# Scores of a graph-attention kernel: keys carried through the folded query matrix instead of a query projection

## The reference, cut to what matters

```python
q_exp = where(x.sum(-1) == 0, 0, cond)             # a zero row of x drops the condition
self_feat = concat([x, q_exp]) @ W_self.T + b_self
output = self_feat
for d in range(2):
    A    = adj[:, :, :20] if d == 0 else swapaxes(adj, 1, 2)[:, :, :20]   # B, N, 20, 11
    mask, vb = A.sum(-1) > 0, A @ w_bias + b_bias
    qh = (self_feat @ Wq[d].T + bq[d])              # B, N, 16, 32
    kh = (self_feat[:, :20] @ Wk[d].T + bk[d])      # B, 20, 16, 32
    aff = einsum('bnhd,bmhd->bnhm', qh, kh) / sqrt(32)
    w = softmax(where(mask, aff, NEG) + vb)         # over the 20 keys
    output += einsum(w, self_feat[:, :20], Wout[d]) + bout[d]
out = x + relu(output)
```

## Time and profile before

| | us |
|---|---|
| time, median of 3 runs (lowest, highest) | 1905.44 (1904.07, 1905.74) |
| the profiled execution, its own time | 1906.23 |
| its span, first to last instruction | 1904.4 |
| mean granted TensorE clock | 0.999 of 2.4 GHz |

### The profile page before, as it was taken

One profiled execution on the slowest core, in us unless ns is written; L12 is line 12 of the kernel. 1 busy time (PEld: TensorE's weight loads), 2 busy tenths in 40 slices (PEclk: granted clock), 3 DMA queues, 4 the chain that ended last, 5 costly groups with the idle time before them and its releaser, 6 DMA issues.

```text
span 1904.4 us, 34516 instructions
## 1 busy us (share of the span) xinstructions
PE 1887.3 (99%) x11020; PEld 1646.9 (86%) x11020; DVE 1303.7 (68%) x1897; ACT 575.5 (30%) x1189; POOL 836.6 (44%) x746
## 2 busy tenths in 40 slices
PE   8999999999999999999999999999999999999999
PEld 6899999888888888888888888888888888888887
DVE  3433232477777777777777777777777777777776
ACT  3333232233333333333333333333333333333332
POOL 0332222354444444444444444444444444444443
PEclk9999999999999999999999999999999999999999
DMA  7123324544444444444444444444444444444431
GB/s 214 34 84 89 96 90 99 136 113 122 122 122 119 118 120 121 121 121 121 121 121 121 121 121 121 121 121 121 121 121 121 121 121 121 121 121 121 121 100 63
DMA packets 227951, 219.87 MB, mean 115 GB/s; under 512 B 58176, under 2 KB 179008, under 8 KB 223808
## 3 DMA queue, kind: packets, MB, share of 16 engines
q1 hardware_dynamic: 223440, 219.24, 42.6%
q10 hardware_dynamic: 4464, 0.02, 0.1%
HBM read 164.39 MB, written 54.79 MB: 115 GB/s over the span
## 4 chain that ended last, share of the span: by engine, by line
PE 95%; DVE 1%; DMA 0%; issue 0%; SPq 0%; POOL 0%; ACT 0%; ACTq 0%; DVEq 0%
PE bank L1517 37%; PE bank L1463 19%; PE bank L849 14%; PE bank L1451 12%; PE bank L1487 8%; PE bank L1476 4%; PE bank L857 0%; PE bank L1436 0%; DMA adj<-in_mask_BxSxSx_ik 0%; PE bank L1526 0%; DVE nodes_t L88 0%; DVE qt_main L1276 0%; SPq L650 0%; DVE nodes_t L1212 0%; POOL rc L1152 0%
## 5 line engine op out<-in xcount | busy, mean ns | idle before, releaser
L1152 POOL TENSOR_TENSOR rc<-nzb,cqg 128x512 f32<-128x512 bf16 x256 | 265.1, 1041 | 419.9 <-DVE qt_main L1276 409.3
L1451 PEld LDWEIGHTS bank<-kbd,qt_main 128*128 128x128 f32 x2048 | 243.6, 192 | 19.1 <-DVE sc L1240 13.2
L1276 DVE SCALAR_TENSOR_TENSOR qt_main<-bank,bq_all,rc 128x512 f32<-128x512 f32 x256 | 190.2, 743 | 89.0 <-PE bank L1517 89.0
L1118 POOL TENSOR_TENSOR sc<-sc,mx 128x640 f32<-128x640 f32 x128 | 163.3, 1276 | 199.1 <-DVE mx L1245 198.7
L1451 PE MATMUL bank<-kbd,qt_main 128*128 128x80 f32 x2048 | 247.4, 274 | 0.2
L1362 ACT ACTIVATE wtt<-bank 128x384 f32<-128x384 f32 (+1 forms) x256 | 111.1, 435 | 381.7 <-PE bank L1476 381.6
L1251 DVE TENSOR_REDUCE sm<-sc 128x32 f32<-128x640 f32 x128 | 104.6, 817 | 162.7 <-ACT sc L1354 162.7
L1517 PE MATMUL bank<-nodes_h,wq_h 128*128 128x512 f32 x512 | 210.1, 410 | 1.9 <-DVE qt_main L1276 1.9
L1517 PE MATMUL bank<-xh_odd,wq_h 128*128 128x512 f32 x512 | 210.5, 411 | 0.0
L1517 PE MATMUL bank<-xh_odd,wq_l 128*128 128x512 f32 x512 | 202.4, 395 | 0.0
L1517 PE MATMUL bank<-nodes_h,wq_l 128*128 128x512 f32 x512 | 202.1, 395 | 0.0
(11 more groups left out here) (130 smaller groups left out, 3816.8 us busy)
## 6 DMA issues: line engine op xcount, KB each, us to landing
rows<-in_x SPq DMA_DIRECT2D x128, 256.0 KB, 5.0
xk<-in_x SPq DMA_DIRECT2D x32, 1024.0 KB, 6.1
res<-c_dram SPq DMA_DIRECT2D x32, 1024.0 KB, 4.7
out<-res SPq DMA_DIRECT2D x128, 256.0 KB, 2.1
adj<-in_mask_BxSxSx_ik SPq DMA_DIRECT2D x32, 440.0 KB, 5.6
adj<-in_mask_BxSxSx_ik SPq DMA_DIRECT2D x128, 110.0 KB
k_dram<-kv_kst SPq DMA_DIRECT2D x64, 160.0 KB, 1.8
v_dram<-kv_vt SPq DMA_DIRECT2D x256, 40.0 KB
```

The lines of the kernel that those rows point to most:

```text
L1118: pool.tensor_tensor(s, s, mx[:, b % 2, :].unsqueeze(2).to_broadcast([P, DIRS * H, NG]), ALU.subtract).then_inc(s_shifted, 1)
L1152: pool.tensor_tensor(rc[:, c % 2, :].rearrange("p (b n) -> p b n", b=G), nzb[:, par, :].rearrange("p (b n) -> p b n", b=G), cqg[:, par, c, ...
L1276: nc.vector.scalar_tensor_tensor(out=qt[:, c, :], in0=bank[c % 2][:], scalar=bq_all[:, c:c + 1], in1=rc[:, c % 2, :], op0=ALU.add, op1=ALU ...
L1451: mm = nc.tensor.matmul(dst, qt[:, c, b * N:b * N + N], kbd[:, c, :, b * NG:b * NG + NG], start=True, stop=True)
```

## The change

Let A be the folded query matrix of a head, 32 query features x 512 features of x. Before, x goes through A and the result meets the keys. After, the keys go through A, and the result, kx, meets x itself. A key of one head has 32 features only, so its matmul uses 32 of the 128 rows of the array, a strip; four heads of one 128-feature block lie on four strips.

- **prepare_weights**: the fold is written the other way round and kept once in fp32 as a_rows (ACT writes chunks 0 and 1, DVE chunks 2 and 3), instead of as wq_h and wq_l.
- **keys_and_values**: the last half no longer loads, turns and splits group 0. SP waits for 16*C on each k_stored and loads the rows of two pairs and two key tiles; DVE turns pair 0.
- **window_loop** replaces main_loop. Its step is a slot of a pair of batches, 64 slots and some at both ends. The 2 x 16 heads are split in 4 units of 8 heads; slot t works on one unit, for a window of 8 batches (4 pairs of ages 0 to 3). Each pair thus meets all four units in four slots. Per slot PE does: 5 generate steps for the next slot's window (step 0: the constants from the condition and the bias, 41 output rows; steps 1 to 4: kx for one 128-feature chunk of x each), each of 2 x 4 fp32 matmuls of 160 columns, strip r into PSUM bank r; 8 score tiles; and for the pair of age 3 and the one before, self features, turned weights and values. ACT copies each step's 1280 columns from PSUM, DVE makes the low part of the constants.
- No query projection, no qt, no POOL condition product (L1152). The final clip goes from DVE to ACT and the last addition from DVE to POOL. The loads are per pair; x comes a third time (xs) for the row sums. Edges stay in groups of 4, one direction per slot.

```diff
 def fold(n):
-    mm = nc.tensor.matmul(bank[6 + n % 2][:], chunk_columns(w1[j], jo), wqt[:, d, j, :],
+    mm = nc.tensor.matmul(bank[6 + n % 2][:], wqt[:, d, j, c * P:c * P + P], w1[j],
...
+def generate(t, step):
+    d, hh = unit(t)
+    lo, hi = window(t)
+    if step == 0:
+        pe.wait_ge(key_loaded[t.par], 16 * (t.half + 1))
+        pe.wait_ge(zl_ready, 2 * (t.n + 1) if t.real() else 2 * PAIRS)
+        if due(t.n):
+            pe.wait_ge(gen_taken, C * t.n)
+    elif step == 1:
+        pe.wait_ge(z_low, t.n + 1)
+    else:
+        pe.wait_ge(gen_taken, C * t.n + step - 1)
+    for c in range(2):
+        o = C * d + 2 * hh + c
+        for r in range(NQ):
+            s = slice(Q * r, Q * r + Q)
+            rhs = key_tile[s, t.par, c, lo * NG:hi * NG]
+            dst = slice(c * UN + lo * NG, c * UN + hi * NG)
+            if step == 0:
+                mm = nc.tensor.matmul(low_banks[0:ZR, r, dst], zl[s, o, :], rhs, start=True, stop=True)
+            else:
+                mm = nc.tensor.matmul(low_banks[:, r, dst], a_rows[s, o, step - 1, :], rhs, start=True, stop=True)
+    mm.then_inc(pe_gen, 1)
...
 def scores(t, a):
...
+    for b in range(2):
+        w = 2 * (AGES - 1 - a) + b
...
+        for j in range(C):
...
+            mm = nc.tensor.matmul(dst, xt[:, j, p.ring + b, :], kx[:, t.par, j, :, :, w, :].rearrange("p r c m -> p c r m"), start=(j == 0), stop=False)
+        mm = nc.tensor.matmul(dst, flags[0:ZR, p.ring + b, :], zc[0:ZR, t.par, :, :, w, :].rearrange("p r c m -> p c r m"), start=False, stop=True)
...
+def constants_low(t):            # DVE
+    dve.wait_ge(z_high, t.n + 1)
...
+    nc.vector.tensor_tensor(o, generated(Q, ZR, lo, hi), o.bitcast(F32), ALU.subtract).then_inc(z_low, 1)
...
+def keys_out(t, j):              # ACT
+    act.wait_ge(pe_gen, STEPS * t.n + 2 + j)
+    lo, hi = window(t)
+    nc.scalar.activation(taken(kx[:, t.par, j], lo, hi), generated(0, P, lo, hi), ACT.Copy).then_inc(gen_taken, 1)
...
+def slot(t):                     # PE
+    soft, late, nxt = t.back(3), t.back(4), t.back(-1)
+    if soft.real():
+        scores(t, 3)
+    if has_window(nxt):
+        generate(nxt, 0)
+    if late.real():
...
+        turn_weights(late, 1, 0)
+    if t.back(2).real():
+        scores(t, 2)
+    if late.real():
+        turn_weights(late, 1, 1)
+    if has_window(nxt):
+        generate(nxt, 1)
+    if late.real():
+        values(late, 1)
+    if t.back(1).real():
+        scores(t, 1)
+    if has_window(nxt):
+        generate(nxt, 2)
+    if soft.real():
+        self_features(soft, 0, range(0, 2))
+        turn_weights(soft, 0, 0)
+        self_features(soft, 0, range(2, C))
+        turn_weights(soft, 0, 1)
+    if has_window(nxt):
+        generate(nxt, 3)
+    if t.real():
+        scores(t, 0)
...
+        flag_rows(nxt)
+    if soft.real():
+        values(soft, 0)
+    if has_window(nxt):
+        generate(nxt, 4)
+    if soft.real():
+        self_features(soft, 1, range(0, C))
...
+def slot(t):                     # DVE
+    if soft.real():
+        add_masks(t, 3)
+        maxima(t, 0)
+        maxima(t, 1)
+    if has_window(nxt):
+        constants_low(nxt)
+    if t.back(2).real():
+        add_masks(t, 2)
...
+    if t.back(1).real():
+        add_masks(t, 1)
...
+            turn_pair(dve, nxt, range(C))
+        nonzero_rows(nxt)
...
+        count_and_weigh(g, t.c % 2)
+    if t.real():
+        add_masks(t, 0)
+    if has_edges(g):
+        total_and_mask(g, t.c % 2)
```

More of the change, by code:

```diff
@@ L923, in main_loop @@
     HM = H * NG
-    NC = DIRS * C
+    NO = DIRS * C
+    EDGE = 4
+    EG = B // EDGE
+    ZR = Q + WIN + 1
     SLOTS = 4
     PARTS = ((0, 3), (3, 5))
[L927 to L947, removed]
+    STEPS = C + 1
+    assert H * WH == NW * P and NW == 5 and AGES == 4 and N == P
@@ L948, in main_loop @@
+    adj0 = sb("adj0", [P, EDGE * NG, L], I32)
+    adj1 = sb("adj1", [EDGE * NG, N, L], I32)
+    sums = sb("sums", [P, 2], F32)
+    nzf = sb("nzf", [P, WIN], F32)
     wb = sb("wb", [P, L], F32)
     bb = sb("bb", [P, 1], F32)
[L950 to L954, removed]
+    vb = sb("vb", [P, N], F32)
+    cn = sb("cn", [P, N], F32)
@@ L1000, in main_loop, with __init__, back, real @@
     wtt_ready = sem("wtt_ready")
+    c_scaled = sem("c_scaled")
     pe_self = sem("pe_self")
     pe_out = sem("pe_out")
+    out_taken = sem("out_taken")
+    clipped = sem("clipped")
     res_ready = sem("res_ready")
-    S0, S1 = bank[2], bank[3]
-    def turn_bank(part, last):
-        return bank[0] if last and part == 1 else bank[7]
+    OUT, TURN = bank[6], bank[7]
+    class Pair:
+        def __init__(self, k, c):
+            self.k, self.c = k, c
+            self.n = 4 * k + c
+            self.half = 2 * k + c // 2
+            self.par = c % 2
+            self.ring = 2 * (c % AGES)
+        def back(self, a):
+            return Pair(self.k, self.c - a)
+        def real(self):
+            return not isinstance(self.k, int) or 0 <= self.n < PAIRS
+    def ages(t):
+        return [a for a in range(AGES - 1, -1, -1) if t.back(a).real()]
+    def scored(t, a):
+        if isinstance(t.k, int):
+            earlier = sum(len(ages(Pair(0, u))) for u in range(t.n))
+            return earlier + len([o for o in ages(t) if o >= a])
+        return 4 * t.n - 2 - a
+    def has_window(t):
+        return not isinstance(t.k, int) or 0 <= t.n < PAIRS + AGES - 1
+    def window(t):
+        ws = [2 * (AGES - 1 - a) for a in ages(t)]
+        return min(ws), max(ws) + 2
+    def generated(first, last, lo, hi):
+        return low_banks[first:last, :, 0:2 * UN].rearrange("p r (c x) -> p r c x", c=2)[:, :, :, lo * NG:hi * NG]
+    def taken(home, lo, hi):
+        return home.rearrange("p r c w m -> p r c (w m)")[:, :, :, lo * NG:hi * NG]
+    def unit(t):
+        u = t.c % 4
+        return u // 2, u % 2
+    def edge_group(t):
+        return (t.n + 2) // 2 if isinstance(t.k, int) else 2 * t.k + (t.c + 2) // 2
+    def has_edges(g):
+        return not isinstance(g, int) or 0 <= g < EG
+    def slots(eng, body, first):
+        for n in range(first, 4):
+            body(Pair(n // 4, n % 4))
+        with eng.Fori(1, PAIRS // 4 - 1) as k:
+            for c in range(4):
+                body(Pair(k, c))
+        for n in range(PAIRS - 4, PAIRS + 4):
+            body(Pair(n // 4, n % 4))
     def value_pieces():
@@ L1034, in sync_program @@
[L1034 to L1047 removed]
+    PIECES = len(list(value_pieces()))
```

990 lines of the change are left out of this document (485 added, 505 removed).

## The result

The changed kernel took 2180.36 us (median of 4; 2172.94 to 2190.0) against 1905.33 for the kernel before on the same chip (1904.07 to 1905.74): ratio 1.1448, 95% interval 1.1402 to 1.1493. It is 275 us slower, where 1853 had been forecast. The profiled execution took 2179.28 us, its span 2177.4.

The account below looks back on a forecast made before the run. PE was taken to bound the kernel: 412 us to the first full slot, 61 slots of 22.7 and a tail of 55 gave a span of 1852, forecast 1853 us; the forecast's own range was 1785 to 1900.

Parts of the forecast that it names:

- The uncertain step: Generated keys on PE: 40 strip matmuls a slot, four strips at once, 2.7 us (bounds 2.7 to 10.9); weakly held.
- Rival 1: Generate steps: only two strips overlap, 1.22 us a step, slot 26.1, kernel 2060 us; 22%.
- rival 2: Generate steps: no overlap or weight loads in series, slot 28.6 to 30.9, kernel 2215 to 2355 us; 12%.
- the score tile: Scores on PE: four fp32 matmuls plus the constants, 1.28 us each, eight a slot 10.3 us (9.3 to 11.6).
- The constants matmul: In each score tile: one fp32r matmul over 41 rows, 0.106 us plus 0.085 for the type change.
- Rival 3: Ten borders between strips and whole array drain: 2.7 us for 0.4, slot 25.0, or 23.9 without loads; 14%.
- Borders of the strips: Ten borders a slot between strip matmuls and whole array: 0.4 us in all (bounds nothing to 1.65).
- kept work: PE work unchanged per slot: self features, values, transposes, flags and mask, together 9.3 us.
- Head and tail: First full slot begins at 412 us, last slots take 55; bounds for both together 25 us either way.
- rival 4: Generate steps wait for evacuation (step 1's wait, ScalarE's copies): one us a slot more, kernel 1914 us; 5%.
- break-even slot: Slot length at which the changed kernel's span equals the 1904.4 us of before: 23.56 us.
- removed work: Query projection and old scores taken off PE: 14.9 us a slot, of which 13.4 come back.

Follow-up runs that it names:

- b_rows64: Kernel before, one of the 12 self-feature matmuls per batch run over 64 of its 128 rows: 1948.7 us, ratio 1.0218.
- a_take_first: Changed kernel, VectorE takes the self features before the edge sums instead of after: 2177.99 us, ratio 1.1433.
- b_unroll: Kernel before with its groups written out, no loop: 1907.35 us, ratio 1.0006.
- a_full_take_unroll: Changed kernel with constants over 128 rows, the earlier VectorE take, and all slots written out, no loop: 1940.82 us, ratio 1.0183.
- b_rows96: Kernel before, one of the 12 self-feature matmuls per batch run over 96 of its 128 rows: 1905.63 us, ratio 0.9993.
- b_loop4: Kernel before with four groups in the loop's body, twice as long, 7 passes for 14: 1923.61 us, ratio 1.0088.
- a_loop8: Changed kernel with eight slots a pass instead of four, 6 jumps for 13: 2155.54 us, ratio 1.1313.
- a_unroll: Changed kernel with all slots written out, no loop: 2124.53 us, ratio 1.1143.
- a_const_out: Changed kernel with the constants' matmul of each score tile left out: 2035.35 us (one run).
- a_full_take: Changed kernel with constants over 128 rows and the earlier VectorE take, loop kept: 2037.03 us, ratio 1.0692.

## Why the prediction was wrong

**The uncertain step was right.** The forecast hung on whether four strips run at once; they do. A step was to take 0.55 to 0.75 us and takes 0.69 and 0.76. Rival 1 wanted 1.2, rival 2 1.7 to 2.2; both are refuted. Within the step at 1206.43 the instructions start in bunches. The timeline of PE of the kernel after, three cuts of 10 to 50 ns, at 1206.55, 1206.70 and 1206.97 (each lists what is in flight then):

```profile
1206.43 0.42 PE L1547 MATMUL low_banks<-key_tile,a_rows 32*128 32x160 f32 x4
1206.43 0.55 PE L1547 MATMUL low_banks<-key_tile,a_rows 32*128 32x160 f32 x8
1206.68 0.58 PE L1547 MATMUL low_banks<-key_tile,a_rows 32*128 32x160 f32 x11
```

Four start together, four more some 0.24 us later. The rows don't say which strip each is on, but the length settles it: 16 instructions at 0.136 on four strips are 0.544. Started in the order that rival 1 supposes, each strip's second half ahead of the next strip, they would take at least 1.22. The Trainium skill, "TensorE: Matmul & The Clock Gate", Part 3, has matmuls start and end in strict program order; if the two halves stand next to each other in the program, as rival 1 took them to, that doesn't hold here. Its 3.07x would have made the five steps an estimated 3.55; they took 3.8 with borders, and 2.37/0.76 is 3.1: here page and trace agree.

**The step that failed is the score tile.** The constants matmul was costed like a full-row one, 0.106 and a type change of 0.085. It cost about 0.43 on the mean of eight tiles (12.1/8 less 1.09); on full rows it costs 0.14 (9.8/8 less 1.09). The bounds given for the tiles, 9.3 to 11.6, did not hold 12.1. The error was one of place. Rival 3 had the mechanism, a drain at a change of array split, and looked for it only at ten borders of generate steps; the 16 borders around the constants' 41 rows were not counted. The loads show it. The timeline of PEld of the kernel after:

```profile
1204.24 0.18 PEld L1568 LDWEIGHTS bank<-zc,flags 41*128 41x128 f32 x1 [0.17 <-issue]
1204.51 1.11 PEld L1567 LDWEIGHTS bank<-kx,xt_main 128*128 128x128 f32 x8
1205.80 0.18 PEld L1568 LDWEIGHTS bank<-zc,flags 41*128 41x128 f32 x1 [0.17 <-issue]
```

The load at 1205.80 starts in the same instant as its matmul, not under the one before, and so does that at 1204.51: 0.20 us lost ahead, and 0.27 to the next start. The Trainium skill, "TensorEngine Tiling (Array Packing)", Key Properties, says that a change of tiling mode drains the engine; b_rows64 agrees, with 0.33 us for two borders. Worth 2.38 us a slot, 133 us in all. It is the largest single term, but it does not turn the sign: with it put right the kernel took 2047, still 7% more than before.

**Borders of the strips** were taken at 0.4 us a slot. Steps are 0.7 over the forecast's 3.1, and kept work, whose blocks stand next to steps, 0.6 over its 9.3 (two value blocks 2.53 for 2.29). Together that is 1.3 us, and with the 0.4 of the forecast 1.7, less than rival 3's upper end of 2.7 and near its 1.65. No experiment splits it further, so that it is the borders is argued, not shown.

**The wait for res** was not in the sum. The prediction looked at waits on generate steps only; this one is at self features of the second batch (L1580), behind total_and_mask on DVE. DVE is 50% busy: an engine with time to spare and the wrong order. It is 0.6 us in the slot shown. Taking it away brought nothing alone (a_take_first) and 10 us on full rows (2046.98 to 2037.03), with the jumps in place; without them it was not tried by itself.

**The loop jump** was no part of the prediction. The kernel before has 13 of them and they cost nothing (b_unroll), so no row there shows it; the longer body brings it in. It is 56 us alone. With the other waits gone it grew to 96: 54.9 of it is idle time, and a part of the rest is the granted clock of 0.50 behind the idle stretch.

**Head and tail** were 36 us over, outside the 25 either way. The waits of the start, timeline of PE of the kernel after:

```profile
372.84 1.09 PE L1547 MATMUL low_banks<-key_tile,a_rows 32*128 32x40 f32 x16 [8.20 <-DVE zc L1255]
386.41 1.16 PE L1547 MATMUL low_banks<-key_tile,a_rows 32*128 32x80 f32 x16 [0.82 <-ACT kx L1428]
```

Step 1 waits for DVE's low constants and the later steps for ACT's copies of the partial windows, with too little PE work beside them to hide it; this is the wait that the prediction had in rival 4. Over these waits the granted clock fell to 0.79 at 340 to 380 and 0.59 at 380 to 400. In full slots that wait hardly shows (17.6 us over L1547 in all): rival 4 is refuted for the loop.

**The sum closes.** Of the 4.7 us a slot that the change missed by, tiles are 1.8, steps and kept work 1.3, the wait for res 0.6, jumps 0.8 (13 slots of 30.3 for 26.68), and 0.3 is what ordinary slots take over the one shown. a_full_take_unroll: slot 3 starts at 427.6, 61 slots of 23.63, tail 68, 1937. It misses 1852 by 57 in the slots (borders, mostly), 16 at the start and 13 at the end. The prediction's break-even slot was 23.56 with its own ends; with these ends it is (1904.4-427.6-68)/61 = 23.10. The 14.9 us of removed work per slot come back almost in full: 9.8 and 3.9 us of new work and 0.6 on what is kept, 14.3 (kept and removed add to 24.2 in the forecast, 0.2 more than a pair took). A slot is 0.35 us shorter than a pair was before, 21 us over 61; the two ends take that and 33 us more (496 us, where 1904.4-61x23.98 = 442 were left for them before). What would take the strip borders away, longer runs of strip matmuls with less in between, was not tried.

## What to carry over

Count the changes of array split along TensorE's order, not only at the new blocks: each matmul of 41 or 64 rows among full ones costs about 0.3 us here, and padding it to all rows with zeros takes that away. A loop that costs nothing can begin to cost when its body grows, so compare instruction bytes and the "issue" waits. Judge an edit with the other waits removed, since a gain can be given back at the next one: the take alone brought nothing. And look at the ends by themselves: the best version has the shorter slot and is slower.

## What the runs showed of the hardware

- Matmuls on four strips of 32 rows run side by side even when each is two instructions: 0.76 us for 16, against 2.37 on one strip.
- One matmul over 64 rows among 128-row ones costs 0.33 us (b_rows64); over 96 rows, nothing (b_rows96: ratio 0.9993, 0.9984 to 1.0003).
- A jump of a long loop body costs 2.9 us (b_loop4) to 3.5 (a_loop8) or 4.3 (56/13, a_unroll), and 7.4 (96/13) once the other waits are gone, where an idle stretch of about 4 us is followed by a granted clock of 0.50, the 1.2 GHz level (a_const_out at 1157, a_full_take at 1261). In the kernel before, with 547 matmuls a pass, the same jump costs nothing (b_unroll: ratio 1.0006).
